# Phase 1 of a windowed-scan and mixture-of-experts kernel: the MLP's second layer in three split products instead of whole fp32 ones

## The reference, cut to what matters

```python
y = _ln(xr, ln2_w, ln2_b)
y = jax.nn.gelu(y @ W1 + b1, approximate=False) @ W2 + b2
return xr + y
...
x = x + _L0_conv_ref(_ln_c(x), ...)
t = _to_tokens(x)
t = t + _L0_ffn_ref(_ln_t(t), ...)
```

## Time and profile before

| what | us |
|---|---|
| three timed runs | 2199.79, 2194.22, 2196.67; median 2196.67 |
| the profiled execution's own time | 2182.92 |
| its span (first to last instruction) | 2181.2 |
| mean granted TensorE clock in it | 0.982 of full speed |
| busy: PE, PEld, DVE, ACT, POOL | 2028.1, 1437.0, 1606.3, 1465.5, 1451.7 |

### The profile page before, as it was taken

One profiled execution on the slowest core, in us unless ns is written; L12 is line 12 of the kernel. 1 busy time (PEld: TensorE's weight loads), 2 busy tenths in 40 slices (PEclk: granted clock), 3 DMA queues, 4 the chain that ended last, 5 costly groups with the idle time before them and its releaser, 6 DMA issues.

```text
span 2181.2 us, 39083 instructions
## 1 busy us (share of the span) xinstructions
PE 2028.1 (93%) x10145; PEld 1437.0 (66%) x10145; DVE 1606.3 (74%) x6863; ACT 1465.5 (67%) x2529; POOL 1451.7 (67%) x1286
## 2 busy tenths in 40 slices
PE   3999999999999999999965999999999999999996
PEld 2656565666666666666644777777777777777775
DVE  5677777777777777777744777777777777777775
ACT  3555555545455555555523888988898888898895
POOL 2366666666666666666553777777777777777776
PEclk9999999999999999999976999999999999999998
DMA  4011111121112111111115666676667667666663
GB/s 161 28 54 58 54 50 62 49 63 47 63 47 63 50 60 52 58 54 44 40 43 188 202 215 206 199 216 207 203 207 211 206 201 213 203 207 214 208 203 94
DMA packets 120721, 272.89 MB, mean 125 GB/s; under 512 B 25702, under 2 KB 34303, under 8 KB 120500
## 3 DMA queue, kind: packets, MB, share of 16 engines
q1 hardware_dynamic: 85680, 209.91, 32.4%
q0 software_dynamic: 32000, 58.87, 7.7%
q10 hardware_dynamic: 2820, 1.61, 0.3%
HBM read 204.28 MB, written 66.98 MB: 124 GB/s over the span
## 4 chain that ended last, share of the span: by engine, by line
PE 52%; POOL 20%; DVE 20%; issue 6%; ACT 1%; DMA 1%; ACTq 0%; SPq 0%; POOLq 0%; DVEq 0%
POOL rstd L396 11%; POOL sorted_rows L405 7%; PE mix_ps L1035 7%; PE mix_ps L1033 6%; PE mix_ps L1034 6%; DVE xr_n L625 4%; PE up_ps L1019 3%; PE turn_ps L1019 3%; PE turn_ps L1020 3%; DVE stats L613 3%; PE up_ps L1020 3%; PE turn_ps L1021 3%; PE up_ps L1021 3%; PE tok_ps L1042 3%; DVE y_lo L701 3%
## 5 line engine op out<-in xcount | busy, mean ns | idle before, releaser
L436 POOL DMA_INDIRECT out<-out_sb,idx x412 | 423.8, 1029 | 263.9 <-DVE out_sb L832 155.4
L788 DVE TENSOR_TENSOR g_lo<-g,g_hi 128x512 fp32r<-128x512 f32 x618 | 420.3, 689 | 207.8 <-ACT g_hi L546 117.7
L405 POOL DMA_INDIRECT sorted_rows<-rows,pos x392 | 421.7, 1076 | 114.1 <-issue 99.9
L546 ACT CAST g_hi<-g 128x512 fp32r<-128x512 f32 x618 | 380.9, 616 | 13.1
L485 ACT ACTIVATE g<-up_ps 128x512 f32<-128x512 f32 x294 | 175.6, 597 | 253.3 <-PE up_ps L891 134.5
L425 POOL TENSOR_TENSOR ex<-euler,rows 128x16 f32<-128x16 f32 x103 | 311.9, 3028 | 14.2 <-DMA rows<-sorted_rows 13.0
L900 PE MATMUL y_ps<-g,d_raw 128*96 128x512 f32 x588 | 298.3, 602 | 0.2 <-ACT y_sb L492 0.2
L396 POOL TENSOR_TENSOR rstd<-var_eps,neg_half 128x8 f32<-128x8 f32 x147 | 248.6, 1691 | 12.2
L1033 PE MATMUL mix_ps<-g_hi,ew 128*96 128x512 f32 x618 | 244.5, 396 | 0.5 <-DVE g_lo L788 0.5
L1035 PE MATMUL mix_ps<-g_lo,ew 128*96 128x512 f32 x618 | 244.2, 395 | 0.0
L1034 PE MATMUL mix_ps<-g_hi,ew 128*96 128x512 f32 x618 | 244.0, 395 | 0.0
(11 more groups left out here) (159 smaller groups left out, 4426.7 us busy)
## 6 DMA issues: line engine op xcount, KB each, us to landing
ew<-expert_w SPq DMA_DIRECT2D x206, 384.0 KB
ew<-expert_w SPq DMA_DIRECT2D x206, 288.5 KB
rows<-sorted_rows SPq DMA_DIRECT2D x103, 394.0 KB
x_in<-in_x SPq DMA_DIRECT2D x49, 384.0 KB
out<-out_sb,idx POOLq DMA_INDIRECT x412
sorted_rows<-rows,pos POOLq DMA_INDIRECT x392
sorted_rows<-pad_rows SPq DMA_DIRECT2D x11, 394.0 KB, 10.4
expert_w<-w_hi SPq DMA_DIRECT2D x4, 192.0 KB, 2.6
```

The lines of the kernel that those rows point to most:

```text
L405: pool.indirect_dma_start(out=sorted_rows[:, :], out_offset=bass.IndirectOffsetOnAxis(ap=pos[:, r, s:s + 1], axis=0), in_=rows[:, r, s, :] ...
L436: pool.indirect_dma_start(out=out_rows, out_offset=bass.IndirectOffsetOnAxis(ap=idx[:, r, s:s + 1], axis=0), in_=out_sb[:, r, s, :], in_of ...
L546: act.copy(g_hi[:, n % PART_RING, :], g[:, n % G_RING, :]).then_inc(hi_done, 1)
L788: dve.tensor_tensor(g_lo[:, n % PART_RING, :], g[:, n % G_RING, :], f(g_hi[:, n % PART_RING, :]), ALU.subtract).then_inc(lo_done, 1)
```

## The change

The second layer of phase 1 gets the form that phase 2 has. ACT copies each activation to `g_hi`, DVE makes `g_lo` from it in a new step `mlp_lo`, placed six times in DVE's list of a period, and `down` makes three fp32r products from `d_hi`, `d_lo`, `g_hi` and `g_lo`. `d_hi` and `d_lo` now hold the MLP's weights too. `gelu` waits for `mlp_lo` instead of for `down`, and `down` for `mlp_lo` instead of for `gelu`.

```diff
@@ ACT @@
-                act.copy(d_hi[:, :, :], d_raw[:, KB:, :]).then_inc(act_prep, 1)
+                act.copy(d_hi[:, :, :], d_raw[:, :, :]).then_inc(act_prep, 1)
...
                 if n >= G_RING:
-                    act.wait_ge(down_done, n - G_RING + 1)
+                    act.wait_ge(mlp_lo_done, n - G_RING + 1)
                 act.activation(g[:, n % G_RING, :], up_ps[:, n % 2, :], ACT.Gelu).then_inc(gelu_done, 1)
+                act.wait_ge(gelu_done, n + 1)
+                if n >= PART_RING:
+                    act.wait_ge(down_done, n - PART_RING + 1)
+                act.copy(g_hi[:, n % PART_RING, :], g[:, n % G_RING, :]).then_inc(mlp_hi_done, 1)
@@ DVE @@
-                dve.tensor_tensor(d_lo[:, :, :], d_raw[:, KB:, :], f(d_hi[:, :, :]), ALU.subtract).then_inc(later_prep, 1)
+                dve.tensor_tensor(d_lo[:, :, :], d_raw[:, :, :], f(d_hi[:, :, :]), ALU.subtract).then_inc(later_prep, 1)
...
+            def mlp_lo(t, u):
+                n = UNITS * t + u
+                dve.wait_ge(mlp_hi_done, n + 1)
+                if n >= PART_RING:
+                    dve.wait_ge(down_done, n - PART_RING + 1)
+                dve.tensor_tensor(g_lo[:, n % PART_RING, :], g[:, n % G_RING, :], f(g_hi[:, n % PART_RING, :]),
+                                  ALU.subtract).then_inc(mlp_lo_done, 1)
...
                 if tile(p - 2):
                     positions(p - 2)
+                if tile(p):
+                    mlp_lo(p, 0)
                 if tile(p - 1):
                     dve.wait_ge(x2_ok, 2 * p)
                     moments(LN_T, p - 1, rows[:, (p - 1) % ROW_RING, :, COL_X2:COL_T])
+                if tile(p):
+                    mlp_lo(p, 1)
                 if tile(p + 3):
...
+                if tile(p):
+                    mlp_lo(p, 2)
                 if tile(p - 1):
                     normalise(LN_T, p - 1, rows[:, (p - 1) % ROW_RING, :, COL_T:COL_BELOW],
...
+                if tile(p):
+                    mlp_lo(p, 3)
                 if tile(r):
                     dve.wait_ge(xr_summed, r + 1)
...
                 if tile(p):
+                    mlp_lo(p, 4)
                     add_x2(p, 0)
                 if tile(r):
                     if r >= 1:
                         dve.wait_ge(xr_turned, r)
                     normalise(LN_R, r, xr_n, xr).then_inc(xr_n_ok, 1)
+                if tile(p):
+                    mlp_lo(p, 5)
                 if tile(p - 1):
                     gate(p - 1)
@@ PE @@
                 if n == 0:
-                    pe.wait_ge(later_loaded, 16 * 5)
-                pe.wait_ge(gelu_done, n + 1)
+                    pe.wait_ge(later_prep, 2)
+                pe.wait_ge(mlp_lo_done, n + 1)
                 if k == 0 and m >= 1:
                     pe.wait_ge(y_copied, m)
-                pe.matmul(y_ps[0:C, :], d_raw[:, k, :], g[:, n % G_RING, :], start=(k == 0), stop=(k == KB - 1)).then_inc(
-                    down_done, 1)
+                part = n % PART_RING
+                pe.matmul(y_ps[0:C, :], d_hi[:, k, :], g_hi[:, part, :], start=(k == 0), stop=False)
+                pe.matmul(y_ps[0:C, :], d_lo[:, k, :], g_hi[:, part, :], start=False, stop=False)
+                pe.matmul(y_ps[0:C, :], d_hi[:, k, :], g_lo[:, part, :], start=False, stop=(k == KB - 1)).then_inc(down_done, 1)
```

More of the change, by code:

```diff
@@ L128, in build_program @@
         d_raw = sb("d_raw", [P, KB * (1 + EXPERTS), C])
-        d_hi = sb("d_hi", [P, KB * EXPERTS, C], F32R)
-        d_lo = sb("d_lo", [P, KB * EXPERTS, C], F32R)
+        d_hi = sb("d_hi", [P, KB * (1 + EXPERTS), C], F32R)
+        d_lo = sb("d_lo", [P, KB * (1 + EXPERTS), C], F32R)
         b2_col = sb("b2_col", [P, 1 + EXPERTS])
@@ L226, in build_program @@
         x_n_ok, x_t_ok, h_t_ok, y_hi_ok = sem("x_n_ok"), sem("x_t_ok"), sem("h_t_ok"), sem("y_hi_ok")
+        mlp_hi_done, mlp_lo_done = sem("mlp_hi_done"), sem("mlp_lo_done")
         gelu_done, y_copied, tn_t_ok = sem("gelu_done"), sem("y_copied"), sem("tn_t_ok")
@@ L291, in _ @@
             for e in range(EXPERTS):
-                r, c, d = slice(e * P, (e + 1) * P), slice(HID * (1 + e), HID * (2 + e)), slice(KB * e, KB * (e + 1))
+                r, c, d = slice(e * P, (e + 1) * P), slice(HID * (1 + e), HID * (2 + e)), slice(KB * (1 + e), KB * (2 + e))
                 for at, src in ((E_HI, f(w_hi[:, c])), (E_LO, f(w_lo[:, c])),
```

## The result

The changed kernel takes 2412.64 us (median of 4 runs, 2410.19 to 2414.83), the kernel before, run beside it, 2198.23 us. The ratio is **1.0975, with a 95% interval from 1.0952 to 1.0999**.

A forecast was written before the change was run, and what follows sets the result against it. The prediction took a chain mainly over DVE and POOL to bound phase 1. It added 48 periods x 5.0 = 240 us to the profiled 2182.9, then 14 for the median of runs, rounded to 2435 us; range 2290 to 2495.

The forecast's parts named there:

- The bound: Phase 1: the chain runs mainly over DVE and POOL, not PE despite its 93% busy share; cheaper products count as nothing.
- DVE and POOL at full clock, +2.4: Phase 1 chain through moments, `rstd`, `xr_n`, `mlp_lo` 5 and `down` 5: next `up` 2.4 us later each period at full clock.
- POOL's hold: POOL's `var_eps` of x waits some 0.5 us for DVE's `mlp_lo` 2, adding 0.3 us to the chain.
- The gap on PE: Ahead of the scores: they wait for `add_x2` behind five `mlp_lo`, so PE idles 1.8 us where it had no gap.
- The clock: PE's clock falls near the scores in nearly every period, slowing later steps: +2.6 us, making +5.0 a period in all.
- +4.6: Case in which PE's clock returns within `from_state`: the period grows by 4.6 us instead of the +5.0 taken.
- the cause given for the fall: PE ahead of the scores: the computed 1.8 us gap, far longer than one seen before a fall, makes the clock fall.
- The clock holds: Rival: PE's clock stays full in phase 1, only DVE's serial work counts, +2.4 us a period, 2312 us; chance 0.30.
- The clock comes back late: Rival: the next tile's `down` and `up` also run at half clock, about 29 us a period, 2528 us; chance 0.07.
- Not slower: Rival: DVE's two waits, 4.59 us, absorb the 3.66 us of subtractions; 2197 us, or down to 2151; chance 0.04.

The follow-up runs named there:

- reordered kernel of before: Kernel before, with DVE's moments of tile p-1 put ahead of positions(p-2), in the wait for the ranks: ratio 0.9683, 20.63 us a period.
- two split units: Kernel before with the moments moved, plus split products for units 3 and 4 only, their subtractions placed in DVE's waits: ratio 0.9665, 20.55 us a period.
- two filled kernels: Changed kernel plus unread PE matmuls: seven ahead of the scores (ratio 1.0900), or these and one behind every second group of the scores (1.0637).
- no subtraction: Changed kernel without `mlp_lo` on DVE, the third product reading `g_hi` instead of `g_lo`: ratio 1.0030, 22.10 us a period.
- fp32 products kept: Changed kernel with copies and subtractions still run, but `down` multiplying whole fp32 `d_raw` and `g`: ratio 1.0882, 25.89 us a period.
- filled kernel: Changed kernel plus seven unread matmuls on PE between the turn of x and the scores: ratio 1.0900, 25.87 us a period.
- both waits used: Changed kernel with `mlp_lo` 4 and 5 in DVE's wait for `rstd` and the moments of tile p-1 in that for the ranks: ratio 1.0174.

## Why the prediction was right

**The bound.** That PE's 93% was no reason to expect a gain held: in no run did the split products bring a gain that could be measured. PE bounds only in the reordered kernel of before, and there two split units gave 0.08 us a period, within the noise.

**DVE and POOL at full clock, +2.4.** The quiet periods of the two filled kernels take 24.40 us, +2.3. The single steps came out close, counted from the period's first `up`: `var_eps` of x took 0.54 us (about 0.5 forecast, 0.19 before), `xr_n` began at 17.56 (17.7 forecast), `mlp_lo` 5 lies behind it, and `down` 5 started at 20.2 (20.3 by the working). That `xr_n` came out so close is in part luck. The forecast added 0.3 for POOL's hold; what the rows show is +0.35 for `var_eps` of x, +0.45 for the third `var_eps` and `rstd` together and -0.65 for the third scatter, which the forecast had kept at 1.61 us or longer.

**The gap on PE.** The scores began at 16.44 (16.5 forecast) behind 1.71 us of idle time (1.8 forecast).

**The clock.** The granted clock fell during the scores or just behind them in nearly every period, and its price was the term that was mis-sized: +2.0 us instead of +2.6, the whole +4.4 instead of +5.0. The turn of `xr_n` started at 21.62 (21.8 forecast), but the clock came back within `from_state`, so the next `up` was at 26.5 and not at 27.1; +4.6 was the case that the working named for this. The end of the path was another, though: the working had the next `up` bound by PE's `from_state`; by the rows it waits 0.27 us for `y_lo`, and `y_lo` stood behind DVE's 2.46 us for `turn_y`. 0.57 x 48 = 27 us is about what the forecast was too high.

**The step that failed** is the cause given for the fall. "The gap that I compute is far longer than that one, so I expect the clock to fall": the fall did come, but with the gap filled it still came in 44 of 48 periods, and in the kernel without subtractions a gap of 0.6 us went with a fall in every second period. The length of the gap isn't without meaning: at gaps of 0.6, 1.2 and 1.7 us (no subtraction, fp32 products kept, changed) there were 85, 217 and 300 us of slow clock. But with the gap filled there were still 233, so the forecast was right on the fall partly by luck. The falls come with the gap, the scores and, in many periods, the wait for `down` 5 behind them; with the gap and the scores both filled, the slow clock went from 300 to 55 us. How much each part weighs was not separated, and what makes the clock fall stays open.

**The rivals.** "The clock holds" gave 2312 us, ratio about 1.052, and falls with the changed kernel's own rows. It is about the right account of what is left at full clock: 2.3 x 48 = 110 us, or 1.050. The Trainium skill (TensorE: Matmul & The Clock Gate, section "Why this matters for your kernels") ties such a fall to one idle gap longer than any here. It didn't hold: the longest gap ahead of the scores was 1.73 us (1.71 in the period shown), and in the filled kernel there was none ahead of the fall shown. "The clock comes back late" needed 29 us a period; none was seen. "Not slower" was right on a part of its one point, that place decides: with both waits used, the change costs 1.9 us a period instead of 4.4, against the old kernel in the same order. It isn't nothing, though, and the clock still falls in 30 periods.

## What to carry to other kernels

Before adding work to an engine, count its idle time by place in its list: 5 us of idle a period hid little here, because they were two fixed waits: 3.66 us of subtractions cost 2.3 at full clock. The same instructions placed by these waits cost 1.9 us a period in all instead of 4.4, and filling one wait in the old kernel gained 3.2%. Compare such a version with the old kernel in the same order, or the gain of the order is counted for the change. Work taken off TensorE can go with a fall of its clock, and then it comes back as half speed for the steps on the chain; so look at the granted clock before and after, not at PE's share.

## What the runs showed of the hardware that was not expected

- The clock fell to half while PE ran with hardly any idle time: 1.87 us of 512-column matmuls, then 4-column scores, and within these the clock went from 1.00 to 0.50 between 710.0 and 710.5.
- More work on PE made the changed kernel faster: fillers by 0.7% in the gap and by 3.1% in the gap and the scores, whole fp32 products instead of split ones by 0.9%. In the order with `mlp_lo` 4 and 5 moved, fillers made it slower, by 1.2%.
- A gap of 0.6 us ahead of the scores, with lighter products, went with a fall in every second period (no subtraction: 85 us at half clock in 1061). The kernel before, without that gap, had one fall, in its last period, behind 0.55 us; two lighter units without a gap had a clock of 1.00.
- POOL's steps that come under a subtraction of DVE take longer: `var_eps` 0.54 us instead of 0.19, and the third `rstd` 1.99 instead of 1.67 (median) in every kernel that has `mlp_lo` 4 just ahead of it, and 1.67 in every one that has it behind `add_x2` or not at all. The other way round nothing is seen: no subtraction of the changed kernel's 294 took longer than 0.69 us, and in the kernel with both waits used 191 of them began within a `rstd` with 0.3 us or more of it to go, none took over 0.74, and these `rstd` took 1.67 as always. The Trainium skill (SBUF — State Buffer, section "Who interferes with whom") has the order of issue decide which of the two blocks; here only POOL was seen to wait.
